# A recurrent and mixture-of-experts kernel: where the shared sweep turns its tokens

## The chip, the core and the metric

The kernel is one program on one core of a Trainium2 chip. The metric is the device time of one execution in microseconds (us), the median of three runs. One execution was also recorded by the hardware profiler. In the code TensorE is `pe`, VectorE `dve`, ScalarE `act`, GpSimd `pool`, and SyncE `sp`, which here only issues transfers. In the profile they are PE, DVE, ACT, POOL and SP.

## The reference

For 8192 tokens of 512 features it computes, cut to what matters:

```python
xn = layernorm(x)                                   # (8, 1024, 512)
s  = recurrence(xn @ W1 + b1) @ W2 + b2             # gated scan over each sequence
shared = (silu(xn @ sgw) * (xn @ suw)) @ sdw        # 512 -> 1024 -> 512
logits = xn @ gate_w                                # 32 experts, top 1
score  = sigmoid(max(logits))
routed = (silu(xs @ rg[e]) * (xs @ ru[e])) @ rd[e]  # xs = xn * score, e = argmax(logits)
out = x + s * silu(shared + routed)
```

## The kernel before, in words

The program has three stages: the shared sweep (`shared_sweep`), then the recurrence, then the routed experts. The change touches the shared sweep alone, which fills about the first 1140 us.

The sweep goes over 16 chunks of 512 tokens; a chunk is 4 tiles of 128 tokens (`q` = 0 to 3). Two chunks stand before a loop, twelve are in it (two for each turn of the loop), two behind it. The layernorm works with a token on each partition, while TensorE needs features on the partitions. So every normalised tile `xn[:, q]` (128 tokens by 512 features) has to be turned, and is then split into two fp32r parts: `xT[j][:, 0]` (rounded, by ScalarE, `x_hi`) and `xT[j][:, 1]` (the rest, by VectorE, `x_lo`). Each product is made of three matmuls over these parts (`matmul_pairs`).

Before the change TensorE turns: `transposes` (L688) makes four 128 by 128 transposes of a tile against the identity matrix into the PSUM tile `psT`, and both halves of the split read `psT`.

In chunk c TensorE's written order is: eight blocks `b`, each of 12 matmuls into `psG` and 12 into `psU` (128 by 512 each), then the router for chunk c+1, then the down product, 4 times 24 matmuls into `psY`. The tiles of chunk c+1 are turned behind blocks 0, 2, 4 and 6 of chunk c (`turned_after`; in chunk 0 behind 2, 3, 5 and 6). VectorE has one step for each block: `h_mul(b)` (L548, needs `psU` of the block), `h_lo(b-1)` (L552), then `x_lo` of a tile (L512) where one was turned, then in blocks 4 to 7 the statistics of chunk c+2 (L489). Behind block 7 come the moments, the copy of the router's result (L519), `normalise` of chunk c+2 (L506, writes `xn`) and `route`. ScalarE does silu (L444), `h_hi(b-1)` (L437) and `x_hi` (L426) for each block. A bank of `psG` or `psU` is written again two blocks later: block b waits for silu and `h_mul` of block b-2.

SyncE issues all transfers of the sweep, in the written order of its `one`: load `x_in` for chunk c+2 (L301), store `xT` of chunk c+1 (L305), then the outputs of the down product (L320) with the store of the scaled tokens (L309) between them. It waits at each for the engine that makes the data. `xq` does not exist before the change; its memory is `raw_weights`, a staging tile that is used only while the shared weights are loaded, in chunk 0.

Of the kernel before, what the change touches and what calls it, by code (L numbers as in the profile page):

```python
# [18 lines left out]
ALU = mybir.AluOpType  # L19
ACT = mybir.ActivationFunctionType  # L20
# [6 lines left out]
P = 128  # L27
CHUNK = 512
TILES = CHUNK // P
# [50 lines left out]
def settle(eng, settled):  # L80

    eng.sem_inc(settled, 1)
# [17 lines left out]
def at_least(eng, sem, value):  # L100

    if not isinstance(value, int) or value > 0:
        eng.wait_ge(sem, value)
# [5 lines left out]
def shared_sweep(nc, z, x, gate_w, sgw, suw, sdw, xT, xT_dram, xs_dram, ss_dram, onehot, ident, tok_dram,  # L109
# [11 lines left out]
    KD, NI, E, D, I, NCH = z.KD, z.NI, z.E, z.D, z.I, z.NCH  # L121
# [3 lines left out]
    with ExitStack() as ctx:  # L125
        k = Kit(nc, ctx)
# [5 lines left out]
        y = k.sb("y_sb", [P, 2, D])  # L132
        assert 2 * D == KD * QC
        raw = [y[:].rearrange("p q d -> p (q d)"), k.sb("raw_weights", [P, KD * QC])[:]]
        order, parts = [], {}

        def part(key, hi_lo, src):
# [9 lines left out]
        for n in range(TILES):  # L147
            cols = slice(n * QC, (n + 1) * QC)
# [7 lines left out]
        xn = k.sb("xn", [P, TILES, D])  # L156
# [47 lines left out]
        def turned(c, q):  # L204

            if isinstance(c, int) and c == 0 and q > 0:
                return (psG[0], psG[1], psU[0])[q - 1][:].rearrange("p (k t) -> p k t", k=KD)
            return psT[:]

        def by_expert(c):  # L210


            if isinstance(c, int) and c == 0:
                return onehot[0:2 * E].rearrange("p t e -> p (t e)")[:, N - 2 * CHUNK:N].bitcast(F32)
            return h[0:2 * E, 0]

        def turned_after(c, b):

            after = (2, 3, 5, 6) if isinstance(c, int) and c == 0 else (0, 2, 4, 6)
            return after.index(b) if b in after else None  # L220

        x0_loaded = [k.sem(f"x0_loaded{q}") for q in range(TILES - 1)]
        x_loaded = [k.sem(f"x_loaded{j}") for j in range(2)]
# [8 lines left out]
        newton = k.sem("newton")  # L232
        xn_done = k.sem("xn_done")
        xpose_done = k.sem("xpose_done")
        xhi_done = k.sem("xhi_done")
        xlo_done = k.sem("xlo_done")
        logits_mm = k.sem("logits_mm")
# [44 lines left out]
        def nxt(c, j, it):  # L282
            return c + 1, 1 - j, it + j

        def nxt2(c, j, it):
            return c + 2, j, it + 1
# [10 lines left out]
        @block.sync  # L297
        def _(sp):
            def load(c, j, it):
                at_least(sp, xs_stored, (c - 1) * 16)  # L300
                sp.dma_start(x_in[:, j], x_v[c]).then_inc(x_loaded[j], 16)  # L301

            def store_xT(c, j, it):
                sp.wait_ge(xlo_done, (c + 1) * TILES)
                sp.dma_start(xT_dram[c], xT[j][:].bitcast(F32)).then_inc(xT_stored[j], 16)  # L305

            def store_xs(c, j, it):
                sp.wait_ge(xs_done, (c + 1) * TILES)
                sp.dma_start(xs_v[c], x_in[:, j]).then_inc(xs_stored, 16)  # L309

            def one(c, j, it, more, more2):
                if more2 and not (isinstance(c, int) and c == 0):
                    load(*nxt2(c, j, it))
                if more:
                    store_xT(*nxt(c, j, it))
                for q in range(TILES):
                    if q == TILES // 2 and more:
                        store_xs(*nxt(c, j, it))
                    sp.wait_ge(y_copied, c * TILES + q + 1)
                    sp.dma_start(ss_t[c * TILES + q][:, 0:D], y[:, q % 2]).then_inc(y_stored[q % 2], 16)  # L320

            for q in range(TILES):
                sp.dma_start(x_in[:, 0, q], x_v[0][:, q]).then_inc((x0_loaded + x_loaded[0:1])[q], 16)
            for n, key in enumerate(order):
                at_least(sp, w_lo, n - 1)
                sp.dma_start(parts[key][2], parts[key][1]).then_inc(w_loaded[key], 16)
                if n == 1:
                    load(1, 1, 0)
            store_xT(0, 0, 0)
            store_xs(0, 0, 0)  # L330
            if NCH > 2:
                load(2, 0, 1)
            sp.wait_ge(sort_const, 4)
            for s0, s1 in ((0, P), (P, z.ROWS)):
                sp.dma_start(tok_dram[s0 * P:s1 * P].rearrange("(s p) a -> s (p a)", p=P),
                             fill[0:s1 - s0]).then_inc(filled, 16)
            sp.dma_start(b1s[:], b1.rearrange("(g p) -> p g", p=P),
                         allow_slow_non_contiguous=True).then_inc(small, 16)
            sp.dma_start(i0[:], init_h.rearrange("(g p) -> p g", p=P),
                         allow_slow_non_contiguous=True).then_inc(small, 16)  # L340
            chunks(sp, one)
            sp.wait_ge(filled, 32)
            sp.wait_ge(small, 32)
            sp.wait_ge(xs_stored, 16 * NCH)
            for j in range(2):
                sp.wait_ge(xT_stored[j], 16 * (NCH // 2))
                sp.wait_ge(y_stored[j], 16 * (NCH * TILES // 2))
# [61 lines left out]
        def _(act):  # L409
# [9 lines left out]
                act.activation(std[:], mv[:, j, :, 1], ACT.Sqrt, bias=eps[:, 0:1]).then_inc(std_done, 1)  # L419

            def x_hi(c, j, it, q):
                act.wait_ge(xpose_done, c * TILES + q + 1)
                if q == 0:
                    at_least(act, xT_stored[j], it * 16)
                    at_least(act, u_mm, (c - 1) * NI)
                act.activation(xT[j][:, 0, :, q * P:(q + 1) * P], turned(c, q), ACT.Copy).then_inc(xhi_done, 1)  # L426

            def scores(c, j, it):
# [45 lines left out]
        def _(dve):  # L474
# [24 lines left out]
            def normalise(c, j, it):  # L499
                dve.wait_ge(std_done, c + 1)  # L500
                at_least(dve, newton, c * 5)
                dve.reciprocal(r0[:], std[:]).then_inc(r0_done, 1)
                dve.wait_ge(newton, c * 5 + 5)
                at_least(dve, xpose_done, c * TILES)
                for q in range(TILES):
                    dve.tensor_scalar(xn[:, q], x_in[:, j, q], mv[:, j, q, 0:1], rstd[:, j, q:q + 1],  # L506
                                      ALU.subtract, ALU.mult).then_inc(xn_done, 1)

            def x_lo(c, j, it, q):
                dve.wait_ge(xhi_done, c * TILES + q + 1)  # L510
                sl = slice(q * P, (q + 1) * P)
                dve.tensor_tensor(xT[j][:, 1, :, sl], turned(c, q), xT[j][:, 0, :, sl], ALU.subtract)\  # L512
                    .then_inc(xlo_done, 1)

# [113 lines left out]
            def one(c, j, it, more, more2):  # L628
                for b in range(NI):
                    if not more:  # L630
                        sort(b)
                    h_mul(c, b)
                    if b >= 1:
                        h_lo(c, b - 1)
                    if b == 2 and isinstance(c, int) and c == 0:
                        route(c, j, it)
                    if more and turned_after(c, b) is not None:
                        x_lo(*nxt(c, j, it), turned_after(c, b))
                    weights(c, b, lo)
                    if isinstance(c, int) and c == 0:  # L640
                        if b == 0:
                            experts_out(c, j, it)
                        elif b == 1:
                            normalise(*nxt(c, j, it))
                    if more2 and b >= NI - TILES and not (isinstance(c, int) and c == 0):
                        stats_of(*nxt2(c, j, it), b - NI + TILES)
                h_lo(c, NI - 1)
                if more2 and isinstance(c, int) and c == 0:
                    for q in range(TILES):
                        stats_of(*nxt2(c, j, it), q)  # L650
                if more2:
                    moments(*nxt2(c, j, it))
                if more:
                    experts_out(*nxt(c, j, it))
                if more2:
                    normalise(*nxt2(c, j, it))
                if more:
                    route(*nxt(c, j, it))
                if not more:
                    slots()  # L660
# [17 lines left out]
        def _(pe):  # L678
# [21 lines left out]

            def turn_logits(c, j, it):
                pe.wait_ge(by_expert_done, c + 1)
                settle(pe, settled)
                for q in range(TILES):
                    mm = pe.transpose(by_token[:, q, :], by_expert(c)[:, q * P:(q + 1) * P], ident[0:2 * E, 0:2 * E])
                mm.then_inc(by_token_done, 1)
# [16 lines left out]
            def one(c, j, it, more, more2):  # L723
                first = isinstance(c, int) and c == 0
                for b in range(NI):
# [10 lines left out]
                        router(c, j, it)  # L736
                    if first and b == 1:
                        turn_logits(c, j, it)
                    if more and turned_after(c, b) is not None:
                        transposes(*nxt(c, j, it), turned_after(c, b))  # L740
                    if not more:
                        sort(b)
# [1050 lines left out]
```

## Time and profile before

| | us |
|---|---|
| median of 3 runs | 3948.08 (3947.24 to 3951.72) |
| the profiled execution's own time | 3948.54 |
| span of its trace | 3946.9 |
| PE busy in the span | 3853.7 (98%) |
| DVE, ACT, POOL busy | 2080.1, 1980.9, 779.1 |
| one chunk of the sweep (start to start) | 70.25 |

The span is what the trace covers, from the first instruction to the last. A matmul's listed duration (0.39 us) overlaps its neighbours', since matmuls are pipelined: what one costs is read from the distance between two starts. A number in square brackets at the end of a row is how long the engine sat idle ahead of it, and the instruction that ended the wait.

### The profile page before, as it was taken

To read this page: it belongs to the slowest core of one execution; us is meant where nothing else is said; L and a number is where in the kernel's file an instruction comes from. 1 tells how busy PE (TensorE), PEld (TensorE's weight loads), DVE (VectorE), ACT (ScalarE), POOL (GpSimd) and SP (SyncE) were. 2 spreads that over 40 slices of the span, in tenths; PEclk is the share of its full clock that TensorE was granted. 3 is DMA by queue.
4 is the path that set the end of the run, shared out by engine and by line. 5 is a ranking of instruction groups with operands and counts; after the bars stand their busy time and mean duration, and the time that the engine had idled before them with its cause. 6 is when DMAs were issued, how large, how long until landed. Compare 5 with 4: busy or idle time off the path is not lost.

```text
span 3946.9 us, 57364 instructions
## 1 busy us (share of the span) xinstructions
PE 3853.7 (98%) x19582; PEld 3291.6 (83%) x19583; DVE 2080.1 (53%) x3042; ACT 1980.9 (50%) x2668; POOL 779.1 (20%) x840
## 2 busy tenths in 40 slices
PE   8999999999989999999999999989999999999998
PEld 6888888888867788888888888878999898999987
DVE  5232322323246755555555555566666767677674
ACT  3222222222227667676776767754445545455453
POOL 2011010110105200000000000023334334343433
PEclk9999999999999999999999999999999999999999
DMA  5122121121112110000001000066667767677673
GB/s 172 64 78 82 69 82 62 78 81 74 64 54 59 48 52 32 32 32 32 32 32 64 32 32 32 21 232 221 220 224 239 258 214 271 231 263 251 223 263 123
DMA packets 273544, 466.41 MB, mean 118 GB/s; under 512 B 25402, under 2 KB 172987, under 8 KB 269636
## 3 DMA queue, kind: packets, MB, share of 16 engines
q1 hardware_dynamic: 235860, 346.48, 25.5%
q0 software_dynamic: 37616, 119.08, 8.7%
q8 instruction: 36, 0.59, 0.1%
q14 instruction: 32, 0.26, 0.0%
HBM read 364.73 MB, written 102.99 MB: 119 GB/s over the span
## 4 chain that ended last, share of the span: by engine, by line
PE 53%; issue 6%; ACT 5%; DVE 5%; DVEq 1%; DMA 1%; ACTq 0%; POOL 0%; SPq 0%; POOLq 0%
PE bank L87 12%; PE bank L89 12%; PE bank L88 12%; PE bank L1718 9%; PE bank L1108 5%; PE bank L1112 3%; ACT whi L1369 2%; DVE th L1603 2%; PE bank L1668 1%; DVEq L1251 1%; ACT thT L1515 1%; DVE yo L1621 1%; DVE hs L988 1%; ACT L955 0%; DMA harmless<-in_L_attn_x,at_x 0%
## 5 line engine op out<-in xcount | busy, mean ns | idle before, releaser
L87 PE MATMUL bank<-txT,whi 128*128 128x256 f32 (+2 forms) x2048 | 615.1, 300 | 12.8 <-DVE th L1603 6.2
L88 PE MATMUL bank<-txT,whi 128*128 128x256 f32 (+2 forms) x2048 | 609.4, 298 | 0.0
L89 PE MATMUL bank<-txT,wlo 128*128 128x256 f32 (+2 forms) x2048 | 609.3, 298 | 0.0
L87 PE MATMUL bank<-xT,w_hi 128*128 128x512 f32 x1536 | 598.2, 389 | 1.8 <-DVE b2all L1013 1.8
L88 PE MATMUL bank<-xT,w_hi 128*128 128x512 f32 x1536 | 598.0, 389 | 0.0
L89 PE MATMUL bank<-xT,w_lo 128*128 128x512 f32 x1536 | 598.0, 389 | 0.0
L1373 DVE TENSOR_TENSOR wlo<-raw,whi 128x2048 fp32r<-128x2048 f32 x186 | 425.8, 2290 | 114.8 <-ACT whi L1369 114.8
L548 DVE TENSOR_TENSOR h_act<-h_act,psU 128x512 f32<-128x512 f32 x128 | 88.1, 688 | 691.1 <-PE psU L89 688.7
L1718 PE MATMUL bank<-whi,thT 128*128 128x512 f32 x1264 | 413.5, 397 | 8.4 <-issue 6.4
L87 PEld LDWEIGHTS bank<-txT,whi 128*128 128x128 f32 x2048 | 390.4, 191 | 19.9 <-DVE th L1603 11.9
L88 PEld LDWEIGHTS bank<-txT,whi 128*128 128x128 f32 x2048 | 390.7, 191 | 1.2
L89 PEld LDWEIGHTS bank<-txT,wlo 128*128 128x128 f32 x2048 | 390.6, 191 | 0.0
L1369 ACT ACTIVATE whi<-raw 128x2048 fp32r<-128x2048 f32 x186 | 353.9, 1903 | 19.3 <-PE bank L1718 15.5
L87 PEld LDWEIGHTS bank<-xT,w_hi 128*128 128x128 f32 x1536 | 288.5, 188 | 63.3 <-DVE b2all L1013 3.3
L88 PEld LDWEIGHTS bank<-xT,w_hi 128*128 128x128 f32 x1536 | 288.7, 188 | 60.2
L89 PEld LDWEIGHTS bank<-xT,w_lo 128*128 128x128 f32 x1536 | 288.7, 188 | 59.9
L1057 DVE SCALAR_TENSOR_TENSOR log_f<-bank,b1s,log_f 128x512 f32<-128x512 f32 x128 | 96.1, 751 | 403.6 <-ACT log_f L950 403.6
L1515 ACT ACTIVATE thT<-th 128x384 fp32r<-128x384 f32 x256 | 134.0, 523 | 340.9 <-DVE th L1603 340.9
L1718 PEld LDWEIGHTS bank<-whi,thT 128*128 128x128 f32 x1264 | 239.1, 189 | 61.2 <-issue 10.1
L901 POOL COPY state<-hs 128x1 f32<-128x1 f32 x128 | 24.0, 187 | 1294.2 <-DVE hs L988 1291.4
L444 ACT ACTIVATE h_act<-psG 128x512 f32<-128x512 f32 x128 | 76.6, 598 | 350.2 <-PE psG L89 350.0
L1718 PE MATMUL bank<-wlo,thT 128*128 128x512 f32 x632 | 248.0, 392 | 0.0
(207 smaller groups left out, 7701.2 us busy)
## 6 DMA issues: line engine op xcount, KB each, us to landing
raw<-in_L_ffn_routed_gate_w SPq DMA_DIRECT2D x124, 512.0 KB, 3.7
raw<-in_L_ffn_routed_up_w SPq DMA_DIRECT2D x124, 512.0 KB, 5.1
raw<-in_L_ffn_routed_down_w SPq DMA_DIRECT2D x124, 512.0 KB, 4.6
xT_dram<-xT SPq DMA_DIRECT2D x16, 2048.0 KB, 6.3
xT<-xT_dram SPq DMA_DIRECT2D x14, 2048.0 KB, 8.0
xs_dram<-x_in SPq DMA_DIRECT2D x16, 1024.0 KB, 4.4
ss_dram<-y_sb SPq DMA_DIRECT2D x64, 256.0 KB, 2.0
ss_dram<-ry SPq DMA_DIRECT2D x64, 256.0 KB, 2.1
```

The costliest lines, as they stand in the source:

```text
L87: pe.matmul(out, w[0], x[0], start=start, stop=False)
L88: pe.matmul(out, w[0], x[1], start=False, stop=False)
L89: return pe.matmul(out, w[1], x[0], start=False, stop=stop)
L548: dve.tensor_tensor(h[:, b % 2], h[:, b % 2], psU[b % 2][:], ALU.mult).then_inc(h_done, 1)
L1057: dve.scalar_tensor_tensor(lf[:], bank(n, 0)[:], bias(GF, kb), lf[:], ALU.add, ALU.min)\
L1108: pe.matmul(psY[q][:], hT[:, 0, q * P:(q + 1) * P], w[:, kb, :], start=kb == 0 and w is w2[0], stop=False)
L1112: mm = pe.matmul(psY[q][:], hT[:, 1, q * P:(q + 1) * P], w2[0][:, kb, :], start=False, stop=kb == NB - 1)
L1369: act.activation(whi[q][:], raw_of(q, e), ACT.Copy).then_inc(whi_done[q], 1)
L1373: dve.tensor_tensor(wlo[q][:], raw_of(q, e), whi[q][:], ALU.subtract).then_inc(wlo_done[q], 1)
L1515: act.activation(hT[:, 0, b], h[b % 2][:], ACT.Copy).then_inc(hhi, 1)
L1603: dve.tensor_tensor(h[b % 2][:], sg[b % 2][:], psU[b % 2][:, 0:PIECE], ALU.mult).then_inc(h_done, 1)
L1718: mm = pe.matmul(psY[g][:], hT[:, a, b, g * P:(g + 1) * P], w[q][:, kb, :], start=b == 0 and a == 0 and w is whi, stop=b == NI - 1 and a == 1)
```

## The change

For chunks 2 to 15 TensorE no longer turns the tiles; chunks 0 and 1 are as before. In its place:

- `normalise` writes each tile of `xn` with its 512 features in another order: four groups `a` of 128, each made of four runs of 32 features.
- SyncE copies inside SBUF. For each half of a chunk (two tiles) it issues 16 transfers (`quarters`), each from 32 partitions by 2 tiles by 128 elements of `xn` to another 32 partitions of `xq`: partition group r and feature group a change places. A transfer carries 32 KB. The first half is issued ahead of the load of `x_in`, the second half behind it, once the first two tiles have been turned.
- VectorE then transposes each tile in blocks of 32 by 32 (`turn`, one instruction of 128 by 512 a tile), from `xq` back into `xn`. It does so in the steps of blocks 1, 2, 4 and 5.
- `x_hi` and `x_lo` read `xn` in SBUF instead of `psT`, in the steps of blocks 2, 3, 5 and 6 instead of 0, 2, 4 and 6.

```diff
+        HALF = TILES // 2
+        xq = raw[1].rearrange("p (q d) -> p q d", q=HALF)
...
+        def late(c):
+            return not (isinstance(c, int) and c < 2)
...
         def turned_after(c, b):
-            after = (2, 3, 5, 6) if isinstance(c, int) and c == 0 else (0, 2, 4, 6)
+            after = (2, 3, 5, 6)
             return after.index(b) if b in after else None
...
+            def quarters(c, n):
+                if n == 0:
+                    sp.wait_ge(xn_done, (c + 1) * TILES)
+                    sp.wait_ge(w_lo, len(order))
+                at_least(sp, quarters_turned, (c - 2) * TILES + n * HALF)
+                for a in range(KD):
+                    for r in range(KD):
+                        dst = xq[a * 32:(a + 1) * 32].rearrange("p q (r n) -> p q r n", r=KD)[:, :, r]
+                        sp.dma_start(dst, xn[r * 32:(r + 1) * 32, n * HALF:(n + 1) * HALF, a * P:(a + 1) * P])\
+                            .then_inc(quarters_loaded[n], 16)
...
             def one(c, j, it, more, more2):
+                if more and late(c + 1):
+                    quarters(c + 1, 0)
                 if more2 and not (isinstance(c, int) and c == 0):
                     load(*nxt2(c, j, it))
+                if more and late(c + 1):
+                    quarters(c + 1, 1)
                 if more:
                     store_xT(*nxt(c, j, it))
...
             def x_hi(c, j, it, q):
-                act.wait_ge(xpose_done, c * TILES + q + 1)
+                if late(c):
+                    act.wait_ge(quarters_turned, (c - 2) * TILES + q + 1)
...
+                if late(c):
+                    act.activation(by_block(xT[j][:, 0, :, q * P:(q + 1) * P]), turned_quarters(q), ACT.Copy)\
+                        .then_inc(xhi_done, 1)
...
                 for q in range(TILES):
+                    if late(c):
+                        dve.tensor_scalar(xn[:, q].rearrange("p (a k i) -> p a k i", a=KD, k=KD),
+                                          by_quarter(x_in[:, j, q]), mv[:, j, q, 0:1], rstd[:, j, q:q + 1],
+                                          ALU.subtract, ALU.mult).then_inc(xn_done, 1)
...
+            def turn(c, j, it, q):
+                dve.wait_ge(quarters_loaded[q // HALF], (c - 1) * 16 * KD * KD)
+                dve.transpose(xn[:, q], xq[:, q % HALF]).then_inc(quarters_turned, 1)
...
+                    if more and late(c + 1) and turned_after(c, b + 1) is not None:
+                        turn(*nxt(c, j, it), turned_after(c, b + 1))
                     if more and turned_after(c, b) is not None:
                         x_lo(*nxt(c, j, it), turned_after(c, b))
...
-                    if more and turned_after(c, b) is not None:
+                    if more and not late(c + 1) and turned_after(c, b) is not None:
                         transposes(*nxt(c, j, it), turned_after(c, b))
```

How the order on two engines changes. SyncE, from the start of a chunk's `one` in the loop (line numbers of each kernel's own code; `raw_weights` is `xq`), before:

```order
L301 ISA [waits xs_stored]
L301 DMA x_in<-in_L_attn_x 128x4x512
L304 REGISTER_ALU
L305 ISA [waits xlo_done]
L305 DMA xT_dram<-xT 128x4096
```

and after:

```order
L103 ISA [waits w_lo,xn_done]
L338 DMA raw_weights<-xn 32x2x128 [waits quarters_turned]
L338 DMA raw_weights<-xn 32x2x128 x15
L103 ISA
L322 ISA [waits xs_stored]
L322 DMA x_in<-in_L_attn_x 128x4x512
L103 REGISTER_ALU
L338 DMA raw_weights<-xn 32x2x128 [waits quarters_turned]
L338 DMA raw_weights<-xn 32x2x128 x15
L326 ISA [waits xlo_done]
L326 DMA xT_dram<-xT 128x4096
```

The load of `x_in` now stands behind 16 transfers, the store of `xT` behind 16 more and a wait for VectorE's second transpose.

VectorE, the steps of blocks 4 and 5 in the loop, before:

```order
L548 TENSOR_TENSOR h_act<-h_act,psU 128x512 [waits u_mm,sg_done]
L552 TENSOR_TENSOR hT<-h_act,hT 128x512 [waits hhi_done]
L510 REGISTER_ALU
L512 TENSOR_TENSOR xT<-psT,xT 128x4x128 [waits xhi_done]
L486 ISA
L103 ISA [waits x_loaded0]
L489 BN_STATS stats<-x_in 128x6 [waits mv_done]
L546 REGISTER_ALU
L548 TENSOR_TENSOR h_act<-h_act,psU 128x512 [waits u_mm,sg_done]
L552 TENSOR_TENSOR hT<-h_act,hT 128x512 [waits hhi_done]
L489 BN_STATS stats<-x_in 128x6
```

and after:

```order
L606 TENSOR_TENSOR h_act<-h_act,psU 128x512 [waits u_mm,sg_done]
L610 TENSOR_TENSOR hT<-h_act,hT 128x512 [waits hhi_done]
L561 STREAM_TRANSPOSE xn<-raw_weights 128x512 [waits quarters_loaded1]
L531 ISA
L103 ISA [waits x_loaded0]
L534 BN_STATS stats<-x_in 128x6 [waits mv_done]
L604 REGISTER_ALU
L606 TENSOR_TENSOR h_act<-h_act,psU 128x512 [waits u_mm,sg_done]
L610 TENSOR_TENSOR hT<-h_act,hT 128x512 [waits hhi_done]
L561 STREAM_TRANSPOSE xn<-raw_weights 128x512 [waits quarters_loaded1]
L564 REGISTER_ALU
L567 TENSOR_TENSOR xT<-xn,xT 128x4x128 [waits xhi_done]
```

A transpose stands in both steps, behind `h_mul` and `h_lo`, and waits for the transfers of the second half; `x_lo` moved from the step of block 4 to that of block 5.

## Rows read from the trace of the kernel before

**Rows 1.** Waits of TensorE in 0 to 1100 us: waited for, us, times, longest.
```profile
PE psT L688 <- DVE xn L506: 11.3, 1, 11.3
PE psT L688 <- DVE logits L525: 1.9, 1, 1.9
PE psG L87 <- DVE xT L512: 1.7, 1, 1.7
PE psT L705 <- DVE h_act L519: 1.5, 1, 1.5
```
**Rows 2.** Stretch of one chunk: busy us by engine, granted clock, DMA share, GB/s.
```profile
312.51:382.76 70.25, 70.25 (x319) 56.91 (x317) 20.79 (x52) 18.21 (x29) 9.48 (x10) 1.00 0.20 77
```
**Rows 3.** Timeline of TensorE around a turn: start, duration, engine, line, tiles.
```profile
334.50 0.39 PE L88 MATMUL psU<-xT,gu_hi 128*128 128x512 f32 x1
334.73 0.39 PE L89 MATMUL psU<-xT,gu_lo 128*128 128x512 f32 x1
334.96 0.60 PE L688 MATMUL psT<-ident,xn 128*128 128x128 f32 x4
335.31 0.48 PE L87 MATMUL psG<-xT,gu_hi 128*128 128x512 f32 x1
335.63 0.39 PE L88 MATMUL psG<-xT,gu_hi 128*128 128x512 f32 x1
```
**Rows 4.** Timeline of VectorE, `h_mul` of blocks 0 to 3 of one chunk.
```profile
312.51 0.69 DVE L548 TENSOR_TENSOR h_act<-h_act,psU 128x512 f32<-128x512 f32 x1 [19.03 <-PE psU L89]
...
318.41 0.69 DVE L548 TENSOR_TENSOR h_act<-h_act,psU 128x512 f32<-128x512 f32 x1 [4.07 <-PE psU L89]
...
323.86 0.69 DVE L548 TENSOR_TENSOR h_act<-h_act,psU 128x512 f32<-128x512 f32 x1 [4.16 <-PE psU L89]
...
329.79 0.69 DVE L548 TENSOR_TENSOR h_act<-h_act,psU 128x512 f32<-128x512 f32 x1 [4.04 <-PE psU L89]
```
**Rows 5.** Groups by line, 0 to 1200 us: count, busy us, mean ns, idle before.
```profile
L552 DVE TENSOR_TENSOR hT<-h_act,hT 128x512 fp32r<-128x512 f32 x128 | 87.5, 684 | 0.2
...
L688 PE MATMUL psT<-ident,xn 128*128 128x128 f32 x244 | 37.0, 274 | 13.2 <-DVE xn L506 11.3 <-DVE logits L525 1.9
...
L426 ACT ACTIVATE xT<-psT 128x512 fp32r<-128x512 f32 x61 | 36.6, 600 | 118.2 <-PE psT L688 118.2
...
L506 DVE TENSOR_SCALAR xn<-x_in,mv,rstd 128x512 f32<-128x512 f32 x64 | 30.7, 543 | 28.1 <-POOL rstd L374 28.1
```
**Rows 6.** Timeline of SyncE's queue: start, time to issue all of the row.
```profile
0.88 1.83 SPq L323 DMA_DIRECT2D x_in<-in_L_attn_x  x4
...
69.88 4.01 SPq L339 DMA_DIRECT2D init_h_by_channel<-in_L_attn_init_h  x1
...
372.50 5.84 SPq L320 DMA_DIRECT2D ss_dram<-y_sb  x2
378.64 0.41 SPq L301 DMA_DIRECT2D x_in<-in_L_attn_x  x1
...
1160.68 2.54 SPq L858 DMA_DIRECT2D raw_spare<-in_L_attn_W  x4
```
**Rows 7.** DMA issues of the execution: count, KB each, median us to landing.
```profile
ss_dram<-y_sb SPq DMA_DIRECT2D x64, 256.0 KB, 2.0
...
x_in<-in_L_attn_x SPq DMA_DIRECT2D x15, 1024.0 KB, 5.3
...
raw_spare<-in_L_attn_W SPq DMA_DIRECT2D x16, 192.0 KB, 3.1
```
**Rows 8.** Timeline of TensorE: a down product, then the next chunk's block 0.
```profile
354.08 0.39 PE L87 MATMUL psY<-dn_hi,hT 128*128 128x512 f32 x1
...
359.44 0.40 PE L89 MATMUL psY<-dn_hi,hT 128*128 128x512 f32 x1
...
377.05 0.39 PE L87 MATMUL psG<-xT,gu_hi 128*128 128x512 f32 x1
...
382.49 0.60 PE L688 MATMUL psT<-ident,xn 128*128 128x128 f32 x4
```

More of the change, by code:

```diff
@@ L208, in turned, with by_quarter, turned_quarters, by_block @@
             return psT[:]
+        def late(c):
+            return not (isinstance(c, int) and c < 2)
+        def by_quarter(row):
+            return row.rearrange("p (k a i) -> p a k i", k=KD, a=KD)
+        def turned_quarters(q):
+            return xn[:, q].rearrange("p (r k j) -> p k r j", r=KD, k=KD)
+        def by_block(cols):
+            return cols.rearrange("p k (r j) -> p k r j", r=KD)
         def by_expert(c):
@@ L217, in turned_after @@
         def turned_after(c, b):
-            after = (2, 3, 5, 6) if isinstance(c, int) and c == 0 else (0, 2, 4, 6)
+            after = (2, 3, 5, 6)
             return after.index(b) if b in after else None
+        assert KD == TILES and D == KD * P and P == KD * 32
         x0_loaded = [k.sem(f"x0_loaded{q}") for q in range(TILES - 1)]
@@ L234, in shared_sweep @@
         xpose_done = k.sem("xpose_done")
+        quarters_loaded = [k.sem(f"quarters_loaded{n}") for n in range(2)]
+        quarters_turned = k.sem("quarters_turned")
         xhi_done = k.sem("xhi_done")
@@ L421, in x_hi @@
             def x_hi(c, j, it, q):
-                act.wait_ge(xpose_done, c * TILES + q + 1)
+                if late(c):
+                    act.wait_ge(quarters_turned, (c - 2) * TILES + q + 1)
+                else:
+                    act.wait_ge(xpose_done, c * TILES + q + 1)
                 if q == 0:
@@ L425, in x_hi @@
                     at_least(act, u_mm, (c - 1) * NI)
+                if late(c):
+                    act.activation(by_block(xT[j][:, 0, :, q * P:(q + 1) * P]), turned_quarters(q), ACT.Copy)\
+                        .then_inc(xhi_done, 1)
+                    return
                 act.activation(xT[j][:, 0, :, q * P:(q + 1) * P], turned(c, q), ACT.Copy).then_inc(xhi_done, 1)
@@ L503, in normalise @@
                 dve.wait_ge(newton, c * 5 + 5)
-                at_least(dve, xpose_done, c * TILES)
+                at_least(dve, xlo_done, c * TILES)
                 for q in range(TILES):
+                    if late(c):
+                        dve.tensor_scalar(xn[:, q].rearrange("p (a k i) -> p a k i", a=KD, k=KD),
+                                          by_quarter(x_in[:, j, q]), mv[:, j, q, 0:1], rstd[:, j, q:q + 1],
+                                          ALU.subtract, ALU.mult).then_inc(xn_done, 1)
+                        continue
                     dve.tensor_scalar(xn[:, q], x_in[:, j, q], mv[:, j, q, 0:1], rstd[:, j, q:q + 1],
                                       ALU.subtract, ALU.mult).then_inc(xn_done, 1)
+            def turn(c, j, it, q):
+                dve.wait_ge(quarters_loaded[q // HALF], (c - 1) * 16 * KD * KD)
+                dve.transpose(xn[:, q], xq[:, q % HALF]).then_inc(quarters_turned, 1)
             def x_lo(c, j, it, q):
@@ L511, in x_lo @@
                 sl = slice(q * P, (q + 1) * P)
+                if late(c):
+                    dve.tensor_tensor(by_block(xT[j][:, 1, :, sl]), turned_quarters(q), by_block(xT[j][:, 0, :, sl]),
+                                      ALU.subtract).then_inc(xlo_done, 1)
+                    return
                 dve.tensor_tensor(xT[j][:, 1, :, sl], turned(c, q), xT[j][:, 0, :, sl], ALU.subtract)\
@@ L702, in turn_logits @@
                 pe.wait_ge(by_expert_done, c + 1)
+                at_least(pe, logits_done, c)
                 settle(pe, settled)
```

## The prediction

> **What bounds the kernel now.** I first read who waited for whom on TensorE in the sweep [rows 1]. There are four waits, together 16.4 us, and each happened once, so none belongs to every chunk. The stretch of one chunk confirms it [rows 2]: 70.25 us long, TensorE busy for 70.25 of them at a granted clock of 1.00, VectorE for 20.79, ScalarE for 18.21, GpSimd for 9.48, the DMA engines for a fifth. So the sweep lasts as long as TensorE's list of instructions, and a microsecond taken out of that list is a microsecond off the time as long as nothing else grows into its place. I then read TensorE's timeline for what a turn costs [rows 3], VectorE's for how much room it has [rows 4], and SyncE's queue with the landing times for whether the new transfers arrive in time [rows 6, 7].
>
> **What is removed.** The transposes' own listed time, 274 ns each [rows 5], is no price, since they overlap. The starts are [rows 3]: the last matmul of a block at 334.73, four transposes from 334.96, the next block's first matmul at 335.31, its second at 335.63. Undisturbed matmuls stand 0.227 us apart (24 from 377.05 to 382.49, 5.44 us) [rows 8], so without the transposes the second would stand at 334.73 + 2 x 0.227 = 335.18. A turn pushes it out by 0.45 us. VectorE's `h_mul`, released by the end of each block, gives the whole effect [rows 4]: 5.90 us from block 0 to 1 (a turn between), 5.45 from 1 to 2 (none), 5.93 from 2 to 3 (a turn). Against 5.44 these are 0.46 and 0.49; the pattern repeats for blocks 4 and 6. A chunk thus holds 2 x 0.46 + 2 x 0.49 = 1.90 us of turning. The turns for chunks 2 to 15 happen in 14 chunks, and 14 x 1.90 = 26.6 us. That is 224 transposes; with 16 of chunk 1 and 4 of chunk 0's first tile they are the 244 recorded on `psT` [rows 5]. If the 0.01 to 0.04 us beyond the push itself stay, it is 14 x 4 x 0.45 = 25.2 us.
>
> **What VectorE and ScalarE get.** Four block transposes of 128 by 512 a chunk. The trace has none. Nearest are VectorE's pass over two SBUF tiles of that shape, 684 ns, and `normalise`, 543 ns as listed [rows 5]; I take 0.69 us, with 0.54 and twice 0.69, 1.4 us, as ends. Ahead of each `h_mul` VectorE sits idle for about 4 us [rows 4] (about 3.4 in the steps that also hold statistics), so 0.69 or 1.4 us disappear there. The fullest step, block 5, holds h_mul, h_lo, transpose, x_lo and statistics: 5 x 0.69 = 3.5 us of 5.44, or 4.2 with the long transpose. `x_hi` and `x_lo` read SBUF instead of PSUM; h_lo from SBUF takes the same 684 ns, so I cost this at nothing. `normalise` now reads in runs of 32 elements; even if each of its four passes grew from 543 to 684 ns, 0.6 us in all, VectorE has 19.03 us of idle time behind it before the next `h_mul` [rows 4]. Without that cover it would be 14 x 0.6 = 8 us.
>
> **What the queue gets.** 32 transfers of 32 KB a chunk. To issue one takes 0.46 us (four in 1.83) to 0.64 us (four in 2.54) [rows 6]; the second has three pieces for each partition, the new ones have two. 16 take 7.3 to 10.2 us, and the last lands 2.0 to 3.1 us later [rows 7]. Follow the chunk that starts at 377.05 [rows 8]. SyncE is free at 372.50 + 5.84 = 378.3 [rows 6]; `xn` was ready long before, in the previous chunk's down product. First half: issued by 385.6 to 388.5, landed by 387.6 to 391.6. VectorE reaches the first transpose behind h_mul(1) and h_lo(0). h_mul(0) runs at 382.7 [rows 8], h_mul(1) 5.44 later at 388.2, the transpose at 389.4. So it waits at most 2.2 us, inside the 4 us of idle time, and h_mul(2) at 393.6 isn't late. The load of `x_in`, before at 378.64, now goes at 389 at the latest and lands 5.3 us later [rows 7] at 394, or 397 if it shares the engines with the quarters; its first reader is the step of block 4, at 405. Second transpose done at 393.6 + 0.6 + 0.6 + 0.7 = 395.5. Second half: issued by 402.8 to 405.7, landed by 404.8 to 408.8. The third transpose stands behind h_mul(4), 404.5, and h_lo(3), at 405.7: a wait of up to 3.1 us, and h_mul(5), at 409.9, is at most 0.3 us late behind the statistics. TensorE needs h_mul(5) only for `psU` of block 7, at 377.05 + 7 x 5.44 + 2.72 = 417.9. x_lo of the last tile ends at 417.3, the router needs it at 377.05 + 43.5 = 420.6. The store of `xT` is issued then as before, ahead of the first output of the down product. Cost of all this on TensorE: nothing, 3 us of slack at the tightest place.
>
> **Sum.** The profiled execution's 3948.54 - 26.6 = 3921.9 us. That execution stands 0.46 us above the median of the runs, so 3921.5 us. Its own range is 3918 to 3926, from 25.2 to 26.6 us of gain and the runs' spread of a few us.
>
> **Rival 1: the transfers come too late, and the kernel is slower.** Place: VectorE's first and third transposes, with `h_mul`, the release of the PSUM banks and the router behind them. Let X be the time per transfer. The path through one chunk is 378.3 + 16X + 2.0, four VectorE instructions up to the second transpose (2.6), again 16X + 2.0, then nine more instructions up to the last x_lo (5.6), against the 420.6 at which the router wants it: 32X + 12.2 must stay under 42.3, so X under 0.94 us. Beyond that each 0.1 us costs 3.2 us a chunk; the 1.9 us gained are used up at X = 1.0. If each transfer waited for the landing of the one before, X = 2.0 [rows 7], the chunk would be 32 x 1.06 = 34 us longer, less 1.9, and 14 of them 449 us: 4397 us. For it: one issue in the queue took 4.01 us [rows 6], of 1024 single elements behind 3072 more; and here each transfer is spread over 32 partitions only. Against it: four transfers issued within 2.54 us land 3.1 us after their own issue, so landings overlap, and those had 384 pieces each, six times the 64 of a quarter.
>
> The trace shows a landing of 2.0 us for 256 KB [rows 7]. The Trainium skill, "DMA: Bandwidth & Descriptors", section "Rules for kernel authors", speaks against this change: transfers under 64 KB pay mostly overhead and should be merged; its section on the anatomy of a DMA gives the fixed part as about 2.0 us. By that figure, paid one after another, the result would be this rival's; paid once for each batch, it is inside the sum above. The overlap in rows 6 and 7 agrees with the second reading.
>
> **Rival 2: TensorE's matmuls get slower.** Matmuls of the down product stand 0.233 us apart (23 steps from 354.08 to 359.44), those of the blocks 0.227 [rows 8]. If more SBUF traffic (quarters, transposes, x_hi and x_lo reading SBUF) brought the blocks' 192 matmuls to the slower pace, a chunk would lose 192 x 0.0063 = 1.2 us, and the gain would be 14 x 0.7 = 10 us: 3938 us. Against it: the block from 377.05 kept its 5.44 us while a load of 1 MB was landing in SBUF, issued at 378.64 [rows 6, 8].
>
> **Rival 3: the turns are hidden anyway.** The change would then give nothing, 3948 us. It would need TensorE to be held by something else; rows 1 and 2 show no such thing.
>
> **Chances.** Forecast 0.83, rival 1 0.08, rival 2 0.06, rival 3 0.03. Of rival 1 some of the weight lies near its threshold, where the time is within 0.2% of before (8 us, about what a measurement of this kernel can tell from no change). So faster 0.88, within 0.2% 0.05, slower 0.07. The range reaches from just below the forecast's own to rival 2: 3915 to 3939.
>
> **What would show it.** Right: no L688 matmul behind chunk 1, 68.35 us from chunk to chunk with TensorE still busy throughout, `h_mul` every 5.44 us, sixteen quarters issued in 7 to 10 us and landed in 2 to 3, VectorE's transposes at 0.5 to 1.4 us, waiting under 4 us for their transfers. Wrong: idle time of TensorE ahead of L87 released by VectorE or ScalarE in every chunk, an issue of more than 0.94 us for a quarter, or blocks longer than 5.44 us.

## The result, and the profile after

The changed kernel takes 3919.3 us (median of 4, 3917.15 to 3920.35), the kernel before 3949.9 (median of 4, 3947.24 to 3952.21): a ratio of 0.9922 with a 95% interval of 0.9905 to 0.9939. Two later comparisons of the same two kernels gave 0.9921 [0.9908, 0.9935] and 0.9925 [0.9912, 0.9939]. The forecast was 3921.5 us. The profiled execution took 3918.78 us, with a span of 3917.1.

The stretch of one chunk in the changed kernel, with the columns of [rows 2]:

```profile
305.42:373.76 68.34, 68.34 (x302) 55.36 (x301) 23.06 (x57) 17.89 (x29) 9.48 (x10) 1.00 0.27 93
```

It is 68.34 us long instead of 70.25, and TensorE is still busy through all of it, with some 16 instructions fewer. VectorE has 2.3 us more, and the DMA engines 27% instead of 20%.

VectorE in that chunk, `h_mul` (L606) of blocks 0 to 5, with the transposes (L561) between them and the statistics behind the third (L534):

```profile
305.42 0.69 DVE L606 TENSOR_TENSOR h_act<-h_act,psU 128x512 f32<-128x512 f32 x1 [19.03 <-PE psU L89]
310.86 0.69 DVE L606 TENSOR_TENSOR h_act<-h_act,psU 128x512 f32<-128x512 f32 x1 [4.75 <-PE psU L89]
...
313.29 0.71 DVE L561 STREAM_TRANSPOSE xn<-raw_weights 128x512 f32<-128x512 f32 x1 [1.14 <-DMA raw_weights<-xn]
316.30 0.69 DVE L606 TENSOR_TENSOR h_act<-h_act,psU 128x512 f32<-128x512 f32 x1 [2.30 <-PE psU L89]
...
317.50 0.71 DVE L561 STREAM_TRANSPOSE xn<-raw_weights 128x512 f32<-128x512 f32 x1
...
321.74 0.69 DVE L606 TENSOR_TENSOR h_act<-h_act,psU 128x512 f32<-128x512 f32 x1 [2.96 <-PE psU L89]
...
327.18 0.69 DVE L606 TENSOR_TENSOR h_act<-h_act,psU 128x512 f32<-128x512 f32 x1 [3.55 <-PE psU L89]
...
329.70 0.71 DVE L561 STREAM_TRANSPOSE xn<-raw_weights 128x512 f32<-128x512 f32 x1 [1.24 <-DMA raw_weights<-xn]
330.34 0.65 DVE L534 BATCH_NORM_STATS2 stats<-x_in 128x6 f32<-128x512 f32 x1
332.62 0.69 DVE L606 TENSOR_TENSOR h_act<-h_act,psU 128x512 f32<-128x512 f32 x1 [1.63 <-PE psU L89]
```

Where [rows 4] had 5.90 and 5.93 us between two `h_mul` with a turn, it is now 5.44 everywhere. The first and the third transpose wait a little over 1 us for their transfers, and 1.63 us of idle time is still left ahead of the next `h_mul`.

SyncE's queue of that chunk (start, time to issue all of the row), and how long the new transfers take to land:

```profile
301.81 10.20 SPq L338 DMA_DIRECT2D raw_weights<-xn  x16
312.30 0.41 SPq L322 DMA_DIRECT2D x_in<-in_L_attn_x  x1
318.23 10.20 SPq L338 DMA_DIRECT2D raw_weights<-xn  x16
```

```profile
raw_weights<-xn SPq DMA_DIRECT2D x448, 32.0 KB, 1.9
```

Sixteen quarters take 10.20 us to issue, 0.64 each, the upper end of [rows 6], and land 1.9 us later, the lower end of [rows 7].

What VectorE waited for, 0 to 1100 us (total, times, longest):

```profile
DVE h_act L606 <- PE psU L89: 597.8, 122, 19.1
DVE xn L561 <- DMA raw_weights<-xn: 30.6, 28, 1.9
```

Of the 56 transposes 28 waited, for 1.1 us on average and never more than 1.9. None of it reached TensorE: its waits in that stretch are the ones of [rows 1] and two, 3.5 us together, in the sorting part of the last chunk. The kernel before has these two as well, 3.5 us at 1122 us, beyond the end of [rows 1].

Where the time went, by the first `h_mul` of chunks 1 and 15 (its start in each profile): before 101.78 and 1085.26, a distance of 983.48 us; after 100.39 and 1057.18, a distance of 956.79. The 14 chunks gave 26.69 us. The profiled executions are 29.76 us apart. Of the other 3 us, 1.4 lie ahead of chunk 1 and 1.7 behind chunk 15.

### The profile page after: what moved, and what is told of

Its sections match the earlier page's. It is cut to its first block, busy times and chain, and to the rows that moved or that the text cites. A ratio compares the mean times of both kernels' runs of the same rounds, so it can differ in the third digit from the quotient of the medians.

```text
span 3917.1 us, 57366 instructions
## 1 busy us (share of the span) xinstructions
PE 3826.1 (98%) x19358; PEld 3269.6 (83%) x19359; DVE 2113.8 (54%) x3098; ACT 1976.1 (50%) x2668; POOL 782.7 (20%) x840
## 4 chain that ended last, share of the span: by engine, by line
PE 53%; issue 6%; ACT 5%; DVE 5%; DVEq 1%; DMA 1%; ACTq 0%; POOL 0%; SPq 0%; POOLq 0%
PE bank L87 12%; PE bank L89 12%; PE bank L88 12%; PE bank L1779 9%; PE bank L1169 5%; PE bank L1173 3%; ACT whi L1430 2%; DVE th L1664 2%; PE bank L1729 1%; DVEq L1312 1%; ACT thT L1576 1%; DVE yo L1682 1%; DVE hs L1049 1%; ACT L1016 0%; DMA harmless<-in_L_attn_x,at_x 0%
## 5 line engine op out<-in xcount | busy, mean ns | idle before, releaser
L87 PE MATMUL bank<-txT,whi 128*128 128x256 f32 (+2 forms) x2048 | 615.1, 300 | 12.9 <-DVE th L1664 6.2
L89 PE MATMUL bank<-txT,wlo 128*128 128x256 f32 (+2 forms) x2048 | 609.3, 298 | 0.0
L87 PE MATMUL bank<-xT,w_hi 128*128 128x512 f32 x1536 | 598.4, 390 | 1.6 <-DVE b2all L1074 1.6
L89 PE MATMUL bank<-xT,w_lo 128*128 128x512 f32 x1536 | 598.2, 389 | 0.0
L606 DVE TENSOR_TENSOR h_act<-h_act,psU 128x512 f32<-128x512 f32 x128 | 88.1, 688 | 604.8 <-PE psU L89 603.6
L87 PEld LDWEIGHTS bank<-txT,whi 128*128 128x128 f32 x2048 | 390.4, 191 | 19.9 <-DVE th L1664 12.0
L89 PEld LDWEIGHTS bank<-txT,wlo 128*128 128x128 f32 x2048 | 390.4, 191 | 0.0
L87 PEld LDWEIGHTS bank<-xT,w_hi 128*128 128x128 f32 x1536 | 289.0, 188 | 63.1 <-DVE b2all L1074 3.2
L89 PEld LDWEIGHTS bank<-xT,w_lo 128*128 128x128 f32 x1536 | 288.8, 188 | 60.0
```

Of the source, the lines that this page charges most:

```text
L87: pe.matmul(out, w[0], x[0], start=start, stop=False)
L89: return pe.matmul(out, w[1], x[0], start=False, stop=stop)
L606: dve.tensor_tensor(h[:, b % 2], h[:, b % 2], psU[b % 2][:], ALU.mult).then_inc(h_done, 1)
```

## The experiments

**The changed kernel again**, as the yardstick for the kernels that follow.

> The changed kernel once more, as the yardstick for the others and for a narrower interval. Theory (the whole gain is the transposes' place in TensorE's list, 14 chunks x 1.90 us = 26.6 us): about 3922 us against 3949, ratio 0.9933; chunk to chunk 68.34 us. Rival (3 us more come from elsewhere, for good): ratio 0.9923 and a second systematic difference outside chunks 1 to 14, in chunk 0 or behind the sweep.

3918.25 us (5 runs) against 3948.55 (15 runs), ratio 0.9921 [0.9908, 0.9935]. In its profile the distance from chunk 1 to chunk 15 is 1058.61 - 101.83 = 956.78 us, the same to 0.01 us. Here chunk 1 begins at 101.83, as late as before: the 1.4 us ahead of it were scatter between executions.

**The additions alone**: the quarters and VectorE's transposes beside TensorE's own. `normalise` and the two splits stay as in the kernel before; what VectorE transposes is read by nobody.

```diff
+                dve.transpose(xq[:, 1 - q % HALF], xq[:, q % HALF]).then_inc(quarters_turned, 1)
...
+                if more and late(c + 1):
+                    quarters(c + 1, 0)
...
+                    if more and late(c + 1) and b in (1, 2, 4, 5):
+                        turn(*nxt(c, j, it), (1, 2, 4, 5).index(b))
```

> The kernel before, with everything added and nothing removed: TensorE still turns every tile, and beside it SyncE issues the 32 quarters a chunk and VectorE runs the four block transposes, whose results nobody reads (they go from one half of xq to the other). Theory (the additions are hidden beside TensorE): chunk to chunk 70.25 us, time within 0.1% of before, 3949 us. Rival (the additions cost something that the removal outweighs): 70.3 to 72 us a chunk, up to 25 us slower.

3948.65 us (11 runs) against 3948.55, ratio 0.9998 [0.9989, 1.0008]. From chunk 1 to 15: 1084.07 - 100.59 = 983.48 us, as before. The additions cost TensorE nothing, though VectorE waited for them (chunks 1 to 14, 100 to 1050 us):

```profile
DVE raw_weights L534 <- DMA raw_weights<-xn: 20.3, 27, 1.7
```

**The removal alone**: the changed kernel with no quarters and, for chunks 2 to 15, no transposes on either engine. The tiles of these chunks then stay unturned and the work behind the sweep is on other values, so only the sweep is read.

```diff
-                if more and late(c + 1):
-                    quarters(c + 1, 0)
...
-                        turn(*nxt(c, j, it), turned_after(c, b + 1))
...
-                    act.wait_ge(quarters_turned, (c - 2) * TILES + q + 1)
+                    act.wait_ge(xn_done, c * TILES + q + 1)
```

> The changed kernel without the quarters and without VectorE's transposes: from chunk 2 on x_hi and x_lo split the tiles as normalise leaves them, so features and tokens are not turned and the routing behind the sweep is of other values. Only the sweep is read, by the distance from chunk to chunk. Theory: 68.34 us, the same as in the changed kernel, since what is left out was hidden. Rival (the quarters or the transposes still hold something up): less than 68.34 us.

Chunk to chunk 376.79 - 308.45 = 68.34 us, and 1060.23 - 103.44 = 956.79 from chunk 1 to 15. Without any turning of these chunks the sweep is no faster than the changed kernel's. The rival that something of the additions still holds it up is excluded. The whole kernel took 3908.47 us, in a single run; since the work behind the sweep is not the same, this time can't be compared.

**TensorE turns every late tile twice.**

```diff
-                for kb in range(KD):
-                    mm = pe.transpose(turned(c, q)[:, kb, :], ...)
+                for _ in range(1 if isinstance(c, int) and c < 2 else 2):
+                    for kb in range(KD):
+                        mm = pe.transpose(turned(c, q)[:, kb, :], ...)
```

> The kernel before, with TensorE's four transposes of a tile made twice, for chunks 2 to 15. Prices the transposes from the other side. Theory (their price is their place in TensorE's list): four more transposes cost their distance of start to start in the same run of small matmuls, about 0.30 to 0.36 us a turn, 17 to 20 us in all, at most 26.6. Rival (the price is mostly a disturbance of the large matmuls on either side, paid once per turn): under 8 us in all.

A chunk became 387.94 - 316.00 = 71.94 us long, 1.69 more than 70.25, so 0.42 us for four more transposes, above my 0.30 to 0.36 and nearly the 0.475 of the first four. TensorE's timeline around one such turn, to be laid beside [rows 3]:

```profile
327.30 0.39 PE L89 MATMUL psU<-xT,gu_lo 128*128 128x512 f32 x1
327.54 1.03 PE L689 MATMUL psT<-ident,xn 128*128 128x128 f32 x8
328.33 0.48 PE L87 MATMUL psG<-xT,gu_hi 128*128 128x512 f32 x1
```

From L89 to L87 it is now 1.03 us, before 0.58. The rival, a disturbance paid once per turn, falls. But the whole kernel took 3992.71 us (4 runs), ratio 1.0107 [1.0091, 1.0122], 44 us more and not 24. The other 20 lie behind the sweep (21.6 us more behind the start of chunk 15 in the profile), in a stage that the edit doesn't touch: the recurrence's loop. Its turns are seen by SyncE's load of `xT`, which comes twice in a turn: 2112.41 to 2290.40 is 178.0 us, before 2075.14 to 2249.22, 174.1. There TensorE stood idle ahead of matmuls for the gates for nothing that the profile shows (releaser `issue`). The rows are of 1378 to 2423 us (count, busy, mean ns, idle before), first in the kernel before, then here, and then one of the waits in the timeline:

```profile
L87 PE MATMUL bank<-xT,w_hi 128*128 128x512 f32 x1152 | 448.1, 389 | 0.0
```


```profile
L87 PE MATMUL bank<-xT,w_hi 128*128 128x512 f32 x1128 | 441.4, 391 | 9.7 <-issue 9.7
```

```profile
1741.59 0.50 PE L87 MATMUL bank<-xT,w_hi 128*128 128x512 f32 x1 [1.92 <-issue]
```

**A longer program, executed once**, to find out why.

```diff
-                for kb in range(KD):
+                for _ in range(17 if isinstance(c, int) and c == 1 and q == 0 else 1):
+                    for kb in range(KD):
```

> The kernel before, with 64 more transposes on TensorE, all in one turn of chunk 1's first tile, executed once. As a program it is as much longer ahead of the recurrence as the kernel that turned every late tile twice, in which a turn of the recurrence's loop went from 174.1 to 178.0 us with TensorE waiting for its own issue. Theory (where the recurrence's loop lies in TensorE's program sets how often it waits for its instructions): 64 x 0.105 = 7 us in chunk 0, and again 178 us a turn of that loop, about 3975 us. Rival (the slower loop came from what the sweep did, heat or clock): 174.1 us a turn, about 3956 us.

3971.05 us (4 runs), ratio 1.0056 [1.0039, 1.0073], 22 us above before. In its profile 3 of them lie ahead of chunk 1 (it starts at 104.93 instead of 101.78; I had expected 7 for the 64 transposes) and 20 behind the start of chunk 15. The recurrence's loop, 1914.83 to 2092.81, takes 178.0 us, and 176.8 for the next turn. The same group of matmuls in it:

```profile
L87 PE MATMUL bank<-xT,w_hi 128*128 128x512 f32 x1135 | 444.3, 391 | 9.8 <-issue 9.8
```

So it is not what the sweep does; 64 more transposes in TensorE's program ahead of the loop are enough. The doubled turns' price in the sweep is 23.8 us (1107.37 - 100.11 = 1007.26 from chunk 1 to 15, against 983.48), the rest is this.

The DMA queue that carries instructions shows what is different in that stretch (1378 to 2423 us: packets, MB, share of 16 engines; the kernel before, the doubled turns, the longer program):

```profile
q8 instruction: 5, 0.08, 0.0%
```

```profile
q8 instruction: 51, 0.84, 0.3%
```

```profile
q8 instruction: 51, 0.84, 0.3%
```

A packet is 16 KB. In the two slow kernels instructions are read in again all through the loop: in the kernel with doubled turns ten packets between 1560 and 1740 us, in the kernel before none. The only one between 1738.5 and 1742 us starts about 0.5 us ahead of the wait of 1.92 us shown above. Over the whole execution the two have 89 packets on this queue, the other ten profiles 34 to 36.

**Every quarter cut in two.**

```diff
-                        sp.dma_start(dst, xn[r * 32:(r + 1) * 32, n * HALF:(n + 1) * HALF, a * P:(a + 1) * P])\
+                        for t in range(HALF):
+                            sp.dma_start(dst[:, t], xn[r * 32:(r + 1) * 32, n * HALF + t, a * P:(a + 1) * P])\
```

> The changed kernel with every quarter cut in two, one transfer for each tile: 64 transfers of 16 KB a chunk instead of 32 of 32 KB, the same bytes. In the changed kernel one quarter is issued in 0.64 us (10.2 us for 16) and lands after 1.9. The slack model of the prediction (first half, 2.6 us of VectorE, second half, 5.6 us, within 42.3 us) gives, if one still takes 0.64 us to issue, 2 x (20.4 + 1.9) + 8.2 = 52.8 us, so 10.5 us too long for a chunk: chunk to chunk 78.8 us, about 4066 us. If an issue costs by its pieces (one for each partition instead of two, as in the first loads, 0.46 us), the sum is 41.6 us, it just fits, and nothing changes. Rival (something other than the issue bounds the transfers): no change in either the issue time of a half or the chunk.

4067.98 us (2 runs), ratio 1.0301 [1.0281, 1.0322]. From chunk 1 to 15, (1203.66 - 100.45) / 14 = 78.8 us a chunk, the figure of the slack model. Between these two shapes the issue costs by the transfer and not by its pieces or bytes:

```profile
335.14 20.16 SPq L340 DMA_DIRECT2D raw_weights<-xn  x32
```

```profile
raw_weights<-xn SPq DMA_DIRECT2D x896, 16.0 KB, 1.8
```

20.16 us for 32, 0.63 each, for half the bytes and half the pieces. And this is how it comes to TensorE (waits of VectorE, then of TensorE, 100 to 1200 us):

```profile
DVE xn L563 <- DMA raw_weights<-xn: 398.3, 28, 18.4
```

```profile
PE psU L87 <- DVE h_act L608: 111.2, 16, 8.7
```

VectorE stands at its transpose waiting for the transfers; behind it in its queue is the `h_mul` that would free the bank `psU`. The waits are not the whole price: from chunk 1 to 15 the kernel is 146.4 us longer than the changed one. In the chunk from 258.27 the granted clock is 0.94 and TensorE is busy for 71.7 us instead of 68.3. The slack model has no term for that.

**Only the first half cut in two.** The same edit for `n == 0` alone.

> The changed kernel with only the first half's quarters cut in two: 32 + 16 transfers a chunk. The slack model at 0.64 us: 20.4 + 1.9 + 2.6 + 10.2 + 1.9 + 5.6 = 42.6 us against 42.3, right at the threshold: 68.3 to 69 us a chunk, 0 to 10 us slower than the changed kernel. Rival (the model leaves out waits, and the changed kernel itself is near its limit): over 71 us a chunk, the gain gone.

3925.83 us (4 runs), ratio 0.9941 [0.9924, 0.9958]; (1060.87 - 98.32) / 14 = 68.75 us a chunk. That is the threshold. From chunk 1 to 15 it is 5.8 us longer than the changed kernel. The profile lists 2.6 us of it as waits of TensorE (100 to 1060 us), the second row being the router's wait for the last `x_lo`; gaps of about 0.3 us between two matmuls, such as the one ahead of `psU` at 325.32, aren't listed.

```profile
PE psU L87 <- DVE h_act L608: 1.7, 3, 0.8
PE psL L759 <- DVE xT L569: 0.9, 2, 0.6
```

**One quarter at a time.**

```diff
                             .then_inc(quarters_loaded[n], 16)
+                        sp.wait_ge(quarters_loaded[n], (c - 2) * 16 * KD * KD + 16 * (a * KD + r + 1))
+                        settle(sp, settled)
```

> The changed kernel with SyncE waiting after each quarter until it has landed. This is rival 1 of the prediction at its far end. By it a quarter takes 1.9 us to land and perhaps 0.2 more until the next is issued: X = 2.1, 32 x 2.1 + 8.2 = 75.4 us against 42.3, so 33 us more a chunk: about 101 us a chunk, 4380 us. Rival (the fixed part of a transfer is not in its landing but in its issue, 0.64 us, which is paid already): under 75 us a chunk.

(`settle` is a count that holds nothing up.)

4352.16 us (2 runs), ratio 1.1021 [1.0999, 1.1043]; (1490.93 - 101.75) / 14 = 99.2 us a chunk, where the model gave 101: 30.9 us more than the changed kernel's chunk instead of 33.

```profile
330.38 32.58 SPq L338 DMA_DIRECT2D raw_weights<-xn  x16
```

16 in 32.58 us, 2.04 each. TensorE's waits from 100 to 1490 us are 367.0 us, all for `h_mul`, and the granted clock is 0.85 in the chunk from 300.22. Rival 1 is a real mechanism of about the size that the prediction gave it: 4397 us there, 4352 here, so 403 us slower than before instead of 449. The changed kernel escapes it only because the landings overlap with the issues.

**The changed kernel, a third time and with the longer program**, side by side, for the 3 to 4 us that the sweep leaves over. The edit is the `range(17 ...)` above, in the changed kernel.

> The changed kernel a third time, on the same chip as the next one, against the kernel before. The sweep's part is settled by now (26.7 us in the profiles). Theory (nothing else changed for good): 26.7 us below before within its interval, 0.9932. Rival (3 to 4 us more come from outside the sweep): 0.9923.

> The changed kernel with 64 more transposes on TensorE in one turn of chunk 1's first tile, executed once: TensorE's program is then as long ahead of the recurrence as in the kernel before the change. The transposes themselves cost 64 x 0.106 = 6.8 us. Theory (the place of the later loops did not matter between before and changed): 6.8 us above the changed kernel of the same call, the recurrence's loop 174.1 us a turn. Rival (the shorter program gave the 3 to 4 us outside the sweep): 10 to 11 us above it.

3920.76 us (5 runs), ratio 0.9925 [0.9912, 0.9939], and 3924.28 (5 runs), 0.9934 [0.9921, 0.9948]. The difference is 3.5 us, less than the 6.8 of the transposes and far from the 10 of the rival; with intervals of 5 us it says no more than that. In the profiles chunk 1 begins 5.3 us later (106.72 against 101.44) and the sweep from chunk 1 to 15 is the same, 956.8 us. The recurrence's loop in the longer one is 1880.76 to 2054.84, 174.1 us, as in both kernels. So the shorter program did not give the left-over microseconds.

## Why the prediction was right

- **What bounds the kernel.** TensorE had no wait in the 14 chunks before and has none after; 26.7 us taken from its list are 26.7 us less. The removal alone gives the whole of it, the additions alone change nothing: 983.48 us from chunk 1 to 15 with and without them.
- **The size.** 14 x 1.90 = 26.6 us was read from [rows 3, 4]; the profiles give 26.69 and, in the second profile of the changed kernel, 26.70. The few hundredths beyond the plain push of 0.45 us went too: the lower sum of 25.2 is out. The medians lie 29 to 31 us apart, 3 to 4 more, where the intervals reach from 24 to 37 us. Taken together, the 35 runs of the kernel before average 3949.5 us and the 14 of the changed one 3919.6: 29.8 apart, with 1.2 to either side at 95%. So about 3 us more than the sweep's are gained, and the prediction has no term for them. The profiles don't show where. Behind the start of chunk 15 the kernel before has 2861.6 us, the changed one 2859.9, 2862.7 and 2860.9; ahead of chunk 1 they are 101.8 against 100.4, 101.8 and 101.4. The length of the program ahead of the recurrence was tried and isn't it. The cause of these 3 us stays open.
- **VectorE and ScalarE.** The transpose takes 708 ns, I took 690. `normalise` in runs of 32 kept its 543 ns, `x_lo` from SBUF takes 668 and `x_hi` 622. All of it is in idle time, as argued.
- **The queue.** 0.64 us an issue was the slow end of my range, and three of the 28 halves went beyond it (10.36 to 10.87 us for 16, at 95.95, 113.21 and 232.85 us). 1.9 us to land is just under the fast end; 2.2 and 3.1 us of waiting were the most I allowed, and it is 1.1 on average and 1.9 at most. The section on the anatomy of a DMA, from which the prediction took the Trainium skill's 2.0 us, describes transfers that GpSimd issues. Here SyncE issues them, and the 1.9 us are these runs' own.
- **Rival 1.** Its path and its threshold of 0.94 us a transfer are confirmed: 32 transfers of 0.64 us cost nothing, 48 of them (0.96 for each of 32) are just beyond it with 0.4 us a chunk, 64 cost 10.5 and 2.04 us each costs 31, where the prediction's 32 x (X - 0.94) gives 35. The lower clock behind such waits, which it left out, is part of what was measured. The Trainium skill, "DMA: Bandwidth & Descriptors", section "Rules for kernel authors", says that transfers under 64 KB are mostly overhead. The runs agree in this sense: 16 KB took 0.63 us of the issuing queue and 32 KB took 0.64. Its conclusion, to merge them, was not tried; with no wait of TensorE left from them there is nothing in this kernel for it to gain but slack.
- **Rival 2.** The 192 matmuls of the blocks keep their 5.44 us a block with the quarters, the transposes and both splits in SBUF beside them.
- **Rival 3.** Excluded by the result, and by the removal alone.

What is left to gain from turning is small: an estimated 1.9 us for chunk 1, whose tiles stay on TensorE because `xq` is in use for loading in chunk 0. That is less than these comparisons can resolve.

## What to carry to other kernels

Where one engine has no idle time at all, an instruction's price is its distance from start to start in that engine's timeline, times its count, and for the sweep this was right to a tenth of a microsecond. The work that replaces it may be clumsier (32 transfers and four transposes for 16 transposes) as long as each step of it has a latest moment; write that chain down as one sum of issue times, landings and instructions, and you also know how far it may be pushed. Many small transfers are paid in the issuing queue, one at a time (0.64 us each here), and their landings overlap. Past the latest moment the price is more than the waiting, since TensorE's clock was lower behind the waits: 146.4 us against 111.2 of waiting with every quarter cut in two.

## What was not expected

- The recurrence's loop takes 174.1 us a turn in the kernel before, in the changed one, with the additions alone and in the changed kernel with the longer program. It takes 176 to 178 in the two whose TensorE program is 64 transposes longer ahead of it than the kernel before, with 9.7 us of waits for its own issue on L87 where there were none. The changed kernel's program is 64 transposes shorter and its loop is as fast as before. A change ahead of a tight loop can cost 20 us in that loop by the length of the program alone, and that must be looked for before a difference is put down to the edit. In both slow kernels 51 packets of instructions of 16 KB each are read in during that stretch instead of 5, and TensorE's waits for its issue come once in a turn. That points to instructions that are fetched anew in each turn; the profile doesn't say whose they are. Why it happens in these two and not in the others, and from which length on, wasn't tried.
- Such a wait costs more than itself. In the kernel with doubled turns, seven matmuls soon behind the wait of 1.92 us that ends at 1741.59 took 0.63 us instead of 0.39, at a distance of 0.43 us instead of 0.23 (TensorE's timeline; then three stretches of it: the last matmuls ahead of the wait, the slow ones, the ones behind them; the granted clock is the number ahead of the DMA share, 1.00 for 2.4 GHz):

```profile
1742.71 0.63 PE L87 MATMUL bank<-xT,w_hi 128*128 128x512 f32 x1
1743.13 0.63 PE L88 MATMUL bank<-xT,w_hi 128*128 128x512 f32 x1
...
1746.03 0.39 PE L87 MATMUL bank<-xT,w_hi 128*128 128x512 f32 x1
1746.26 0.39 PE L88 MATMUL bank<-xT,w_hi 128*128 128x512 f32 x1
```

```profile
1738.71:1739.66 0.95, 0.95 (x4) 0.48 (x3) 0.83 (x2) 0.95 (x2) 0.00 (x0) 1.00 0.07 17
1742.28:1745.27 2.99, 2.99 (x9) 2.30 (x7) 0.00 (x0) 0.00 (x0) 0.00 (x0) 0.50 0.02 5
1746.03:1750.79 4.76, 4.76 (x22) 3.94 (x21) 0.69 (x1) 3.17 (x5) 0.00 (x0) 1.00 0.00 0
```

The clock was at its lower level, 1.2 GHz, for 3 us behind a wait of 1.9, from within 0.7 us of its end.

- Four more transposes in a row cost nearly as much as the first four (0.42 against 0.475 us), so most of a turn's price is the transposes themselves, about 0.105 us each, and little is the break between the large matmuls.
